# Splitting the issue of the key placements between the sync queue and ScalarE's queue in the first seven steps of a cross-attention kernel

## The chip, the cores and the metric

The kernel runs on one core of one Trainium2 chip. The metric is the device time of one execution in microseconds (us), lower is better, as the median of several runs.

## The reference, cut to what matters

One layer of a small perceiver: cross-attention of 128 queries to 12,544 keys, then a linear attention, a causal self-attention and a mixture of 8 experts, all on 128 rows of width 256. Only the first part bears on the change:

```python
q = query_states @ Wq.T + bq        # 128 x 256
k = key_value_states @ Wk.T + bk    # 12544 x 256
v = key_value_states @ Wv.T + bv
# 16 heads of 16
scores = jnp.einsum('bhqd,bhkd->bhqk', q, k)
attn = jax.nn.softmax(scores, axis=-1)
ctx = jnp.einsum('bhqk,bhkd->bhqd', attn, v)
```

## The kernel before, in words

Each engine has one program, written out by hand, and the engines meet at semaphores; every queue works in order. The keys are worked through in 49 steps (`NS`) of 256 keys (`SK`). `t` counts the rounds of the main loop: in round t TensorE computes the maximum scores of step t (`max_scores`, L568) and, `LAG` = 5 rounds later, the real scores (`scores`, L592) and the weighted values (L608). Rounds 0 to 4 therefore have no real scores, no exponentials and no weighted values yet. Projections run ahead: the values of step t+2 (`values`, L551) and the keys of step t+3 (`keys`, L540) are interleaved in round t.

Numbers are split in two parts, a high and a low one, so that a pass in fp32r keeps the precision. The way of the keys of step n is this:

- `context_high` (ScalarE, L361) and `context_low` (GpSimd, L314) split the context of step n in two parts. TensorE projects it into `k_bank`. In round t it stops before its sixth `max_scores` matmul for the low part of the context of step t+3 (`cl_ready`).
- `keys_high` (ScalarE, L371) and `keys_low` (VectorE, L907) write the high and the low part of the keys to `kst[n % 2]`, 128 partitions: rows 0 to 63 belong to the even heads (a = 0), rows 64 to 127 to the odd ones (a = 1).
- `keys_place` (L232 to L244) moves them by DMA into `kT[n % 7]`, where the 16 dimensions of eight head pairs lie on 16 partitions: for each half a three DMAs, of parts high, low, high, to partitions 64a, 64a+16 and 64a+32 on. A DMA moves 128 KB, so a step takes six of them, 768 KB. They all count up `kt_load{n % 2}`, and 96 of it mean that a step is placed.

`kst` has two buffers: `keys_high(n)` waits until the placement of step n-2 has landed. `max_scores` of step n waits for the placement of step n (`keys_placed`, in rounds before 5; from then on it stands in front of `scores`, L591). The placement also waits until GpSimd has filled its buffer of `kT` with ones (`key_ones`, L320, `pool_kt`), and from step 7 on until the scores that read the buffer before are done. VectorE reduces each of the eight pairs of maximum scores (`step_max`, L923), with `keys_low(t + 2)` between the second and the third. ScalarE's order in rounds 0 to 4 is `keys_high(t + 2)`, `values_out(t + 2)` (L381, rounds 0 to 3), `context_high(t + 4)`. The sync queue's (SP's) order in a round is one load of context (`ctx_load`, L230, 256 KB from HBM), after every fourth step the rows of the maxima (`max_rows`, L255), and `keys_place(t + 2)`.

Of the kernel before, what the change touches and what calls it, by code (L numbers as in the profile page):

```python
# [5 lines left out]
F32 = mybir.dt.float32  # L6
# [10 lines left out]
HD = D // H  # L17
# [7 lines left out]
LAG = BS + 1  # L25
LAST = NS - 1 + LAG
RING = 7
# [29 lines left out]
def last_step(b):  # L57
    return min(b * BS + BS, NS) - 1
# [46 lines left out]
def perceiver_layer(nc, dr, out):  # L105
    ctx = ExitStack()
    with ctx:
# [3 lines left out]
        S = {n: ctx.enter_context(nc.semaphore(n)) for n in COUNTING + ONCE + LOADS + ["dve_chain"]}  # L111
# [28 lines left out]
        def place(name, shape, dt=F32):  # L140
            size = 4
            for n in shape[1:]:
                size *= n
            h = nc.alloc_sbuf_tensor_at(name, shape, dt, offset=at[0])
            at[0] += (size + 31) // 32 * 32
            assert at[0] <= arena_end, (name, at[0] - arena_end)
            return h

        kT = place("kT", [P, RING, PAIRS, SK], F32R)
# [11 lines left out]
        kst = [place(f"kst{i}", [P, 2, 2 * SK], F32R) for i in range(2)]  # L161
# [60 lines left out]
        def _(sp):  # L222
# [9 lines left out]
            def keys_place(n):  # L232


                sp.wait_ge(S["kl_ready"], n + 1)
                sp.wait_ge(S["pool_kt"], min(n + 1, RING))
                if n >= RING:
                    sp.wait_ge(S["sc_done"], 8 * (n - RING) + 8)
                for a in range(2):
                    for seg, part in enumerate((0, 1, 0)):  # L240
                        row = 64 * a + HD * seg
                        sp.dma_start(kT[row:row + HD, n % RING, :, :].bitcast(F32).rearrange("d (i t) k -> d i (t k)", t=2),  # L242
                                     kst[n % 2][64 * a:64 * a + 64, part, :].bitcast(F32)
                                     ).then_inc(S[f"kt_load{n % 2}"], 16)  # L244
# [27 lines left out]
            for t in range(-2, NS + 1):  # L272
                if CRING <= t + 6 < NS:
                    ctx_load(t + 6)
                for b in range(NB):
                    if t == last_step(b) + 1:
                        max_rows(b)
                if t + 2 < NS:
                    keys_place(t + 2)
                if t == LAG:  # L280
                    sp.dma_start(biases[:, early:], dr["biases"][early:].partition_broadcast(P)).then_inc(S["ld_small"], 16)
                    sp.dma_start(router[:, :, :], dr["router"].rearrange("(c p) n -> p c n", p=P)).then_inc(S["ld_small"], 16)
                    sp.dma_start(freqs[:, :], dr["freqs"][0:P, :]).then_inc(S["ld_small"], 16)
                    sp.dma_start(const[:, P:], dr["const"][:, P:]).then_inc(S["ld_small"], 16)
                if t == NS - 2:

                    sp.wait_ge(S["v_done"], 2 * NS)
                    for name in WEIGHTS[3:]:
                        sp.dma_start(*weight(name)).then_inc(S["ld_tail"], 16)
# [65 lines left out]
        def _(act):  # L355
            def context_high(n):

                act.wait_ge(S[f"ld_ctx{n % CRING}"], 16 * (n // CRING) + 16)
                if n >= 2:
                    act.wait_ge(S["v_done"], 2 * (n - 2) + 2)  # L360
                act.activation(cparts[n % 2][:, 0, :, :], ctxT[n % CRING][:, :, :], ACT.Copy  # L361
                               ).then_inc(S["ch_ready"], 1)

            def keys_high(n):


                act.wait_ge(S["k_done"], n + 1)
                if n >= 2:
                    act.wait_ge(S[f"kt_load{n % 2}"], 96 * (n // 2))
                for t in range(2):  # L370
                    last = act.activation(kst[n % 2][:, 0, t * SK:(t + 1) * SK], k_bank[:, t * SK:(t + 1) * SK],  # L371
                                          ACT.Identity, bias=kbias[:, t:t + 1])
                last.then_inc(S["kh_ready"], 1)

            def values_out(n):


                act.wait_ge(S["v_done"], 2 * n + 2)
                if n >= VRING:
                    act.wait_ge(S["pv_done"], 2 * (n - VRING) + 2)  # L380
                act.activation(val[:, n % VRING, :, :, 0:HD].rearrange("p j h d -> p (j h) d"),  # L381
                               v_bank[:, :].rearrange("p (g d) -> p g d", d=HD), ACT.Copy).then_inc(S["val_ready"], 1)

            def exponential(n, q):


                k = 8 * n + q
                act.wait_ge(S["sc_done"], k + 1)
                if k >= PROBS:
                    act.wait_ge(S["pv_done"], (k - PROBS) // GROUPS + 1)  # L390
                act.activation(probs[k % PROBS][:, :, :], sc_bank[k % 3][:, :].rearrange("p (h q) -> p h q", q=P),  # L391
                               ACT.Exp).then_inc(S["exp_ready"], 1)

            def part_out(b):

                act.wait_ge(S["pv_done"], 2 * last_step(b) + 2)
                act.activation(parts[:, b, :], pv_bank[:, :], ACT.Copy).then_inc(S["part_ready"], 1)
# [7 lines left out]
            keys_high(0)  # L405
            act.wait_ge(S["ld_v"], 16)
            act.activation(wv[:, 0, :, :], w["xv"][:, :, :], ACT.Copy).then_inc(S["act_wkvh"], 1)
            keys_high(1)
            act.wait_ge(S["pool_setup"], 1)
            act.wait_ge(S["pe_qT"], 2)  # L410
# [4 lines left out]
            last.then_inc(S["act_q0"], 1)  # L415
            values_out(0)
            context_high(2)
            values_out(1)
            context_high(3)
            for t in range(LAST + 2):  # L420
                for q in range(8):
                    n = t - LAG
                    if 0 <= n < NS:
                        exponential(n, q)
                    if q == 0 and t + 2 < NS:
                        keys_high(t + 2)
                    if q == 5 and t + 2 <= LAG:
                        values_out(t + 2)
                    if q == 5 and t + 4 < NS:
                        context_high(t + 4)  # L430
                    if q == 2:
                        for b in range(NB):
                            if n - 1 == last_step(b):
                                part_out(b)
                    if t == NS + 1 and q == 2:

                        act.wait_ge(S["dve_dmax"], 1)
                        act.activation(bmax[:, :, :], bmax[:, :, :], ACT.Exp).then_inc(S["act_bw"], 1)
# [841 lines left out]
```

## Time and profile before

| | us |
|---|---|
| median of 3 runs | 580.96 |
| lowest, highest | 579.13, 583.05 |
| the profiled execution, its own time | 582.39 |
| span of the profiled execution | 580.60 |

The profiled execution is 1.43 us above the median, within the range of the three runs, and 1.79 us of it lie outside the span. Times in the rows count from the start of the span. PE is TensorE's matmuls, PEld its weight loads, DVE VectorE, ACT ScalarE, POOL GpSimd, SPq the sync queue. Round 0 begins at 21.36 us, round 5 at 54.15 us, and the last round of the key loop ends near 472 us.

### The profile page before, as it was taken

Reading aid. Unit: us, or ns where it says so; the run is one execution under the profiler, and the core shown is the slowest. Engines: PE = TensorE matmul, PEld = TensorE weight load, DVE = VectorE, ACT = ScalarE, POOL = GpSimd, SP = SyncE. Lnnn points to the kernel's source line nnn. Section 1 sums busy time; section 2 is a strip of 40 time slices with the busy share of each in tenths; the row PEclk is TensorE's granted clock in tenths of the full one; section 3 lists DMA queues with packets and bytes.
Section 4 is the critical chain, followed back from the end, with each engine's and each line's share of the span. In section 5 each row is a group of like instructions: output and inputs, shape, how many; then the busy total and the mean of one; then the engine's idle time right before and its main releaser. Section 6 shows DMA issues by size and latency. Waiting matters only on the chain.

```text
span 580.6 us, 15874 instructions
## 1 busy us (share of the span) xinstructions
PE 548.3 (94%) x6517; PEld 507.2 (87%) x6517; DVE 421.7 (73%) x804; ACT 331.4 (57%) x636; POOL 91.8 (16%) x75
## 2 busy tenths in 40 slices
PE   7888989999999999999999999999989998768897
PEld 7777989999999999999999999999977897736686
DVE  5699868778778778787787787787773247866674
ACT  3423747667667667667666676676666740062463
POOL 7741101111011011011011110110000000015000
PEclk9999999999999999999999999999999999988899
DMA  6999996766877877876768768777483029900000
GB/s 193 151 162 151 190 147 103 119 125 117 127 118 116 126 121 114 131 121 114 130 119 121 124 117 127 118 114 101 89 163 101 3 98 371 374 29 1 1 0 9
DMA packets 44651, 70.46 MB, mean 121 GB/s; under 512 B 6788, under 2 KB 15140, under 8 KB 44452
## 3 DMA queue, kind: packets, MB, share of 16 engines
q1 hardware_dynamic: 44580, 69.47, 64.8%
q8 instruction: 50, 0.82, 0.8%
q14 instruction: 21, 0.17, 0.1%
HBM read 30.56 MB, written 0.13 MB: 53 GB/s over the span
## 4 chain that ended last, share of the span: by engine, by line
PE 78%; DVE 10%; DMA 6%; SPq 3%; ACT 2%; issue 1%; DVEq 0%; ACTq 0%
PE bank L592 17%; PE bank L608 15%; PE bank L568 14%; PE bank L551 10%; PE bank L540 10%; DMA kT<-kst 5%; PE bank L811 3%; PE bank L827 3%; SPq L242 2%; DVE stepmax L923 2%; PE bank L616 1%; PE bank L630 1%; DMA ctxT<-in_ctxT 1%; PE bank L520 1%; DVE kst L907 1%
## 5 line engine op out<-in xcount | busy, mean ns | idle before, releaser
L923 DVE TENSOR_REDUCE stepmax<-bank 128x2 f32<-128x512 f32 x392 | 262.9, 687 | 91.6 <-PE bank L568 68.5
L391 ACT ACTIVATE probs<-bank 128x512 f32<-128x512 f32 x392 | 230.8, 599 | 141.9 <-PE bank L592 137.5
L592 PE MATMUL bank<-qmat,kT 128*128 128x256 f32 x784 | 163.5, 293 | 4.5 <-DMA kT<-kst 3.0
L568 PE MATMUL bank<-kT,qM 128*128 128x256 f32 x784 | 161.1, 287 | 4.9 <-DMA kT<-kst 2.6
L592 PEld LDWEIGHTS bank<-qmat,kT 128*128 128x128 f32 x784 | 120.3, 191 | 18.4 <-issue 10.1
L568 PEld LDWEIGHTS bank<-kT,qM 128*128 128x128 f32 x784 | 121.4, 191 | 8.9 <-DVE stepmax L923 4.5
L314 POOL TENSOR_TENSOR cparts<-ctxT,cparts 128x512 fp32r<-128x512 f32 x49 | 63.1, 1288 | 326.2 <-ACT cparts L361 326.2
L540 PE MATMUL bank<-cparts,wk 128*128 128x256 f32 x588 | 101.1, 283 | 1.6 <-DVE kst L907 1.3
L551 PE MATMUL bank<-wv,cparts 128*128 128x256 f32 x588 | 101.9, 284 | 0.7 <-ACT val L381 0.7
L608 PE MATMUL bank<-probs,val 128*17 128x128 f32 x3136 | 95.1, 273 | 0.0
L608 PEld LDWEIGHTS bank<-probs,val 128*17 128x17 f32 x3136 | 81.4, 97 | 6.5
L540 PEld LDWEIGHTS bank<-cparts,wk 128*128 128x128 f32 x588 | 83.8, 192 | 2.3 <-POOL cparts L314 2.1
L551 PEld LDWEIGHTS bank<-wv,cparts 128*128 128x128 f32 x588 | 83.9, 191 | 0.9 <-ACT val L381 0.9
L371 ACT ACTIVATE kst<-bank,kbias 128x256 fp32r<-128x256 f32 x98 | 40.8, 472 | 14.1 <-DMA kT<-kst 11.9
L907 DVE SCALAR_TENSOR_TENSOR kst<-bank,kbias,kst 128x256 fp32r<-128x256 f32 x98 | 42.5, 475 | 3.8 <-ACT kst L371 3.8
L361 ACT ACTIVATE cparts<-ctxT 128x512 fp32r<-128x512 f32 x49 | 30.5, 622 | 6.1 <-PE bank L551 3.3
L917 DVE COPY val<-bank 128x512 f32<-128x512 f32 x43 | 29.2, 680 | 0.0
L350 POOL TENSOR_TENSOR low<-w,high 128x512 fp32r<-128x512 f32 x8 | 10.0, 1292 | 111.9 <-ACT high L464 111.9
L811 PE MATMUL bank<-high,tparts 128*128 128x512 f32 x64 | 19.6, 428 | 0.2 <-DVE tparts L1148 0.2
L616 PE MATMUL bank<-const 128*128 128x128 f32 x136 | 19.2, 289 | 0.0
L1187 DVE TENSOR_TENSOR low<-w,high 128x1024 f32 (+1 forms) x12 | 14.7, 1221 | 5.9 <-ACT high L464 5.9
L616 PEld LDWEIGHTS bank<-const 128*128 128x128 f32 x136 | 18.2, 204 | 0.3
(188 smaller groups left out, 323.4 us busy)
## 6 DMA issues: line engine op xcount, KB each, us to landing
kT<-kst SPq DMA_DIRECT2D x294, 128.0 KB, 4.6
ctxT<-in_ctxT SPq DMA_DIRECT2D x49, 256.0 KB, 5.4
w<-in_w SPq DMA_DIRECT2D x24, 512.0 KB, 10.1
bias<-in_biases SPq DMA_DIRECT2D x1, 1024.0 KB, 6.7
qmat<-maxT SPq DMA_DIRECT2D x26, 8.0 KB
w_xk<-in_w_xk SPq DMA_DIRECT2D x1, 256.0 KB, 3.4
w_xq<-in_w_xq SPq DMA_DIRECT2D x1, 256.0 KB, 3.5
bias<-in_biases SPq DMA_DIRECT2D x1, 256.0 KB, 5.4
```

Of the source, the lines that this page charges most:

```text
L314: pool.tensor_tensor(cparts[n % 2][:, 1, :, :], ctxT[n % CRING][:, :, :], cparts[n % 2][:, 0, :, :].bitcast(F32), ALU.subtract).then_inc(S ...
L371: last = act.activation(kst[n % 2][:, 0, t * SK:(t + 1) * SK], k_bank[:, t * SK:(t + 1) * SK], ACT.Identity, bias=kbias[:, t:t + 1])
L391: act.activation(probs[k % PROBS][:, :, :], sc_bank[k % 3][:, :].rearrange("p (h q) -> p h q", q=P), ACT.Exp).then_inc(S["exp_ready"], 1)
L540: last = pe.matmul(k_bank[:, t * SK:(t + 1) * SK], wk[:, pw, c, t * P:(t + 1) * P], cparts[n % 2][:, pc, c, :], start=(i == 0), stop=(i == 5))
L551: last = pe.matmul(v_bank[:, j * D:(j + 1) * D], cparts[n % 2][:, pc, c, j * P:(j + 1) * P], wv[:, pw, c, :], start=(i == 0), stop=(i == 5))
L568: last = pe.matmul(mx_bank[p % 2][:, a * SK:(a + 1) * SK], qM[:, p, a, :], kT[:, n % RING, p, :], start=True, stop=True)
L592: last = pe.matmul(sc_bank[k % 3][:, i * 2 * P:(i + 1) * 2 * P], kT[:, n % RING, p, j * P:(j + 1) * P], qmat[b % 2][:, p, :, :], start=Tru ...
L608: last = pe.matmul(pv_bank[32 * r:32 * r + VW, g * P:(g + 1) * P], val[:, n % VRING, j, GH * g + r, :], probs[(GROUPS * ch + g) % PROBS][: ...
L616: pe.matmul(B[6][:, 0:P], ident, ident, start=True, stop=True)
L811: last = pe.matmul(B[2 * which + i][:, :], tparts[:, a, c, :], weights, start=(n == 0), stop=(n == len(products) - 1))
L907: last = dve.scalar_tensor_tensor(kst[n % 2][:, 1, cols], k_bank[:, cols], kbias[:, t:t + 1], kst[n % 2][:, 0, cols].bitcast(F32), ALU.add ...
L923: dve.tensor_reduce(stepmax[:, n % BS, 2 * p:2 * p + 2], mx_bank[p % 2][:, :].rearrange("p (a k) -> p a k", a=2), AX_X, ALU.max).then_inc( ...
```

## The change

In the placements of steps 0 to 6, the three DMAs of the odd heads (a = 1) are issued by ScalarE's queue and the three of the even heads stay on the sync queue. From step 7 on the sync queue issues all six as before. Bytes, shapes, destinations and semaphore counts are the same. On ScalarE the new function stands between activations: for step 0 after the copy of the value weights (L407), for step 1 after `context_high(2)`, and for steps 2 to 6 in rounds 0 to 4 behind `keys_high(t + 2)` and ahead of `values_out(t + 2)` and `context_high(t + 4)`. It waits for `kl_ready` and `pool_kt`, as the sync queue does.

```diff
@@ keys_place, sync queue
-                for a in range(2):
+                for a in range(1 if n < LAG + 2 else 2):
@@ ScalarE
+            def keys_place_half(n):
+                act.wait_ge(S["kl_ready"], n + 1)
+                act.wait_ge(S["pool_kt"], min(n + 1, RING))
+                for seg, part in enumerate((0, 1, 0)):
+                    row = 64 + HD * seg
+                    act.dma_start(kT[row:row + HD, n % RING, :, :].bitcast(F32).rearrange("d (i t) k -> d i (t k)", t=2),
+                                  kst[n % 2][64:128, part, :].bitcast(F32)).then_inc(S[f"kt_load{n % 2}"], 16)
@@ ScalarE, before the loop
             act.activation(wv[:, 0, :, :], w["xv"][:, :, :], ACT.Copy).then_inc(S["act_wkvh"], 1)
+            keys_place_half(0)
             keys_high(1)
...
             context_high(2)
+            keys_place_half(1)
             values_out(1)
@@ ScalarE, in the loop
                     if q == 0 and t + 2 < NS:
                         keys_high(t + 2)
+                    if q == 2 and t < LAG:
+                        keys_place_half(t + 2)
                     if q == 5 and t + 2 <= LAG:
                         values_out(t + 2)
```

## Rows read from the trace of the kernel before

**Rows 1.** The page: span, busy shares, and the strips in 40 slices.

```profile
span 580.6 us, 15874 instructions
PE 548.3 (94%) x6517; PEld 507.2 (87%) x6517; DVE 421.7 (73%) x804; ACT 331.4 (57%) x636; POOL 91.8 (16%) x75
...
PE   7888989999999999999999999999989998768897
...
PEclk9999999999999999999999999999999999988899
```

**Rows 2.** Busy time in stretches: a weight load, rounds 0 to 4, a late round.

```profile
core 0: us, PE busy (x) PEld busy (x) DVE busy (x) ACT busy (x) POOL busy (x), PEclk, DMA share, GB/s
8.00:10.00 2.00, 1.91 (x16) 1.75 (x15) 0.00 (x0) 0.23 (x1) 1.93 (x2) 1.00 1.05 377
...
21.36:28.20 6.84, 5.45 (x40) 4.98 (x41) 5.84 (x10) 1.90 (x4) 6.84 (x5) 1.00 1.08 153
28.20:34.95 6.75, 5.49 (x40) 5.02 (x40) 5.85 (x10) 1.96 (x4) 5.28 (x4) 1.00 1.06 155
34.95:41.16 6.21, 5.49 (x40) 5.01 (x40) 5.66 (x10) 1.95 (x4) 1.54 (x2) 1.00 1.08 170
41.16:47.62 6.46, 5.49 (x41) 5.00 (x41) 6.06 (x12) 1.96 (x4) 1.29 (x1) 1.00 1.08 166
47.62:54.15 6.53, 5.56 (x41) 5.18 (x42) 6.14 (x15) 1.47 (x3) 1.29 (x1) 1.00 0.87 140
204.47:213.25 8.78, 8.78 (x123) 8.44 (x122) 6.72 (x12) 5.80 (x12) 1.29 (x2) 1.00 0.80 122
```

**Rows 3.** The chain that ended last, 12 to 80 us: start, us, what.

```profile
17.31 0.55 SPq L242
...
21.11 7.04 DMA kT<-kst
...
28.74 1.29 DVE stepmax L923 x2
30.03 0.79 DVE kst L907 x2
...
34.00 7.12 DMA kT<-kst
...
43.77 3.78 DVE stepmax L923 x6
...
73.20 7.73 DMA kT<-kst
```

**Rows 4.** Timeline of round 1 and the edges of its neighbours: start, us; idle before in brackets.

```profile
28.24 0.84 ACT L371 ACTIVATE kst<-bank,kbias 128x256 fp32r<-128x256 f32 x2 [3.02 <-DMA kT<-kst]
28.74 1.29 DVE L923 TENSOR_REDUCE stepmax<-bank 128x2 f32<-128x512 f32 x2 [1.03 <-PE bank L568]
29.95 0.87 DVE L907 SCALAR_TENSOR_TENSOR kst<-bank,kbias,kst 128x256 fp32r<-128x256 f32 x2
30.84 3.83 SPq L242 DMA_DIRECT2D kT<-kst  x6
30.98 0.60 ACT L381 ACTIVATE val<-bank 128x512 f32<-128x512 f32 x1 [1.90 <-PE bank L551]
31.48 0.62 ACT L361 ACTIVATE cparts<-ctxT 128x512 fp32r<-128x512 f32 x1
32.17 1.28 POOL L314 TENSOR_TENSOR cparts<-ctxT,cparts 128x512 fp32r<-128x512 f32 x1 [1.47 <-ACT cparts L361]
34.95 0.50 PE L568 MATMUL bank<-kT,qM 128*128 128x256 f32 x2 [0.74 <-DMA kT<-kst]
35.49 1.29 DVE L923 TENSOR_REDUCE stepmax<-bank 128x2 f32<-128x512 f32 x2 [0.91 <-PE bank L568]
36.25 0.49 PE L568 MATMUL bank<-kT,qM 128*128 128x256 f32 x2
41.70 1.29 DVE L923 TENSOR_REDUCE stepmax<-bank 128x2 f32<-128x512 f32 x2 [0.36 <-PE bank L568]
```

**Rows 5.** The tile kst, 15 to 55 us: issue ns min/median/max; landing.

```profile
L242 SPq DMA_DIRECT2D kT<-kst x36: 547/598/1720, 14.7 to 54.6; - x36
...
DMA to landing us min/median/max: 3.3/5.9/7.8
```

## Prediction

> **What bounds the kernel now.** I read the page first. TensorE's matmuls are busy for 94% of the span, at the full granted clock in all but the last slices, and the one visibly thinner part of the key loop is its beginning [rows 1]. Then the windows by round. A late round takes 8.78 us with TensorE busy for all of it; there a placement is hidden and the change does nothing, since it ends with step 6. Rounds 0 to 4 are 6.84, 6.75, 6.21, 6.46 and 6.53 us long with TensorE busy for only about 5.5 us of each, so something else sets them. The column before the last tells what: the DMA engines have a share above 1 in rounds 0 to 3, so they never run dry, at 153, 155, 170 and 166 GB/s, and fall to 0.87 in round 4 [rows 2].
>
> The chain of waits gives the order. It goes from the issue of step 1's placement to its landing, 7.04 us after the last of six issues; then over TensorE to two reductions and `keys_low(3)` on VectorE, to the issue of step 3's placement, and to its landing, 7.12 us after the last issue. From 41.7 us on it stays on VectorE [rows 3]. So in rounds 0 and 1 the bound is a loop: placement lands, `keys_high` and `keys_low` fill the freed buffer, the next placement is issued and lands. From round 3 it is VectorE, busy 6.06 us of 6.46 [rows 2].
>
> The timeline prices it. VectorE stands idle for want of a placed step 1.03 us before round 1, 0.91 before round 2 and 0.36 before round 3 [rows 4], 2.30 us in all. That is the most that earlier landings in these rounds can return; below it VectorE's eight reductions and two halves of `keys_low`, 5.66 to 5.85 us a round [rows 2], take over.
>
> **The change part by part.** Removed from the sync queue: 7 x 3 = 21 issues at a median 0.60 us [rows 5]. Six in a row take 3.83 us [rows 4], so with three on each queue the last one is issued some 1.9 us earlier. But the landing isn't the issue plus a constant. One issue of this kind lands 3.3 us after it when nothing is ahead, 5.9 in the median and up to 7.8 [rows 5], and the last of a step takes 7 in the chain [rows 3]: the difference is a queue in front of the DMA engines. While their share is above 1, issuing earlier only makes the queue longer. At nothing, therefore, I put the 1.9 us itself; what covers it is the backlog. In round 4, where the share is 0.87, the cover is gone, but there VectorE is the bound, and the placement of step 6 isn't needed before round 6.
>
> What can change is the pace of the DMA engines. The same engines moved 377 GB/s when they loaded weights from HBM to all partitions, and 153 to 155 when three quarters of their bytes were placements (768 KB of 1 MB in a round), at the same share [rows 2]. So in a placement they are busy waiting: its writes go to 16 partitions at a time, those of one half a for three DMAs on end. With two queues, placements to partitions 0 to 47 and to 64 to 111 are in flight together, and a context load on the sync queue can run beside odd-head placements. The low end of this effect is nothing. The high end is that the stalls end, 2.30 us, for which a round of 6.84 us must shrink to about 5.9, 16% more pace. The nearest rows are rounds 2 and 3, with the same work at 170 and 166 GB/s. I take 170 for rounds 0 and 1: 6.84 x 153/170 = 6.16, saves 0.68; 6.75 x 155/170 = 6.15, saves 0.60; and of round 2's 0.36 I count 0.3, as it then meets VectorE. Sum 1.6 us.
>
> Added to ScalarE: 21 issues and a wait for `keys_low` in each of rounds 0 to 4. Queued behind it are `values_out(t + 2)` and `context_high(t + 4)`; TensorE waits for the first at the start of the next round, and GpSimd, and through it TensorE, for the second. No row shows an issue on ScalarE. By the issues on the sync queue it costs 0.55 to 1.72 us, median 0.60 [rows 5]; I take the median, because both queues do the same instruction, so 3 x 0.64 with the gaps, 1.9 us. In round 1 ScalarE would be through at 30.84 + 1.9 = 32.7 instead of beginning `values_out` at 30.98, and end it at 33.3, `context_high` at 34.0, and GpSimd's half at 35.3. TensorE wants the values at about 35.2, behind the first maximum scores of the next round, and the context part in the third pair, which begins at 36.25 [rows 4]. Both are ready, by 1.9 and about 1.1 us, and with a next round that starts 0.4 us earlier still by 1.5 and 0.7. ScalarE has the room: it is busy 1.96 us of 6.75 [rows 2]. Cost nothing; the cover is TensorE's own work, and it breaks at about 1.0 us an issue (below).
>
> Steps 0 and 1 are placed before the loop. Half of step 0 goes out from ScalarE with `keys_high(1)` behind it, and half of step 1 behind `context_high(2)`, some 0.6 us after the sync queue's half, which still is before the time at which the sixth issue went out. Nothing for either. Rounds from 5 on: ScalarE and the sync queue have their old programs, TensorE is the bound, and what was won or lost before shifts them as a whole. The late landing in the chain at 73 us is that of step 8 behind a group of small loads [rows 3]; it is untouched and moves with the rest.
>
> Sum: -1.6 us. The profiled execution would take 582.39 - 1.6 = 580.8; on the median of the runs, 1.43 lower, it is 580.96 - 1.6 = 579.4.
>
> **The Trainium skill on this.** "SBUF — State Buffer", section "Can I just issue two DMAs to hit both halves?", says no: all DMAs run on the same 16 engines, and two at once, one at partition 0 and one at 64, gained only 6%. "DMA: Bandwidth & Descriptors", section "Issuing engines are not separate DMA queues", adds that a second issuing engine saves only the sequencer's time. Their plain form is the second case below. The trace supports the first half of it (one saturated set of engines) and can't show the other, as all its DMAs but instruction loads are in one queue. With the 6% the rounds would be 6.45 and 6.37 us, an estimate of about 1.1 us saved in place of 1.6.
>
> **The rivals.** (a) Faster pace, the forecast: 579.4, from 578.4 with all 2.3 us and a little at the start of round 0, to 580.4 with a third of it. (b) Hidden anyway: two rings, one set of engines, the same pace, and the placements land when they did. For it: a share above 1 from 21 to 47 us. Against: 377 against 153 GB/s at that share. It gives 581.0. (c) Slower, through ScalarE: two queues that issue at the same moment may take turns, so that an issue takes twice as long, 1.28 us, and three 3.84. Then ScalarE is free at 34.68, the context's high part ends at 35.9 and the low one at 37.25, and TensorE, due at about 36.5 for the second matmul of the third pair, waits 0.8 us in each of the rounds 1 to 4; with `keys_high` of the next round late by as much, that is 3.4 us, 584.4. It decides from (36.5 - 30.84 - 0.60 - 0.62 - 1.29 - 0.1) / 3 = 1.0 us an issue. At the longest single issue, 1.72 us [rows 5], it would be 2.1 us a round, 589.4. For it: the 1.72 exists. Against: it is one of 36, the median is 0.60.
>
> **How the numbers follow.** (a) 0.50, (b) 0.28, (c) 0.20, of which 0.04 at or above the longer price, and 0.02 for what I haven't thought of. One per cent is 5.8 us, about what a measurement of this kernel can tell from no change, as the three runs are 3.9 us apart. (a) and (b) lie wholly within it, and (c) at its likely price too. So faster by over 1% 0.02 (the last case), within 1% 0.94, slower 0.04. The range goes from (a)'s upper gain, less 1.1 us for the scatter of a median, to (c)'s likely price: 577.3 to 584.4; outside it are the long form of (c) and scatter.
>
> **What would show it.** In the profile after, rounds 0 and 1 should be near 6.15 us, with 165 to 175 GB/s in them, and VectorE's idle time before rounds 1, 2 and 3 should sum to under 1 us instead of 2.30. ScalarE's three issues should take about 1.9 us, and `context_low` should still end before the third pair of the next round. The time from the last issue to the landing should rise where (b) holds, to about 9 us, with rounds of 6.8 and 6.75. Under (c) issues on both queues take 1.2 us or more and TensorE's wait for `cparts` (GpSimd, L314) appears in rounds 1 to 4. I would be wrong beyond the range if ScalarE's issues blocked on the backlog of the DMA engines, or if rounds from 5 on changed their 8.78 us.

## The result, and the profile after

| | before | after |
|---|---|---|
| median, us | 582.35 (579.07 to 585.60, 16 runs) | 585.86 (583.13 to 589.74, 16 runs) |
| ratio, 95% interval | | 1.007 (1.0049 to 1.0091) |
| span of the profiled execution, us | 580.60 | 586.20 |

The change costs 0.7% by the ratio; the two medians are 3.5 us apart. The forecast was a gain of 1.6 us. The profiled execution of after, 587.97 us, lies 2.1 us above its own median, so its 5.6 us of longer span are more than the change costs.

The windows by round, of the changed kernel; columns as in [rows 2]. The windows are rounds 0 to 5, then the stretch from round 8's first scores to round 9's, then a late round:

```profile
21.09:27.93 6.84, 5.53 (x42) 4.98 (x41) 5.85 (x10) 1.96 (x4) 5.91 (x5) 1.00 1.07 154
27.93:34.40 6.47, 5.50 (x40) 5.00 (x40) 5.85 (x10) 1.96 (x4) 4.37 (x4) 1.00 1.06 158
34.40:40.34 5.94, 5.41 (x41) 5.04 (x41) 5.39 (x10) 1.96 (x4) 2.57 (x2) 1.00 1.09 178
40.34:46.72 6.38, 5.52 (x41) 5.04 (x40) 6.30 (x11) 1.96 (x4) 1.70 (x2) 1.00 1.07 173
46.72:56.47 9.75, 5.80 (x42) 5.16 (x42) 7.66 (x16) 1.47 (x3) 2.17 (x2) 1.00 1.06 168
56.47:64.78 8.31, 8.31 (x57) 8.31 (x57) 6.08 (x11) 5.61 (x11) 0.89 (x1) 0.79 0.19 36
82.34:95.01 12.67, 10.53 (x123) 9.82 (x122) 7.60 (x18) 5.91 (x12) 1.28 (x2) 0.87 0.48 97
209.00:217.78 8.78, 8.78 (x123) 8.44 (x122) 6.73 (x12) 5.80 (x12) 1.29 (x2) 1.00 0.80 123
```

Rounds 1, 2 and 3 are 0.28, 0.27 and 0.08 us shorter than in [rows 2], and a late round is unchanged. Round 4 is 9.75 us in place of 6.53, and its DMA share is 1.06 in place of 0.87. Round 5 is 8.31 us with TensorE busy for all of it, at a mean granted clock of 0.79; before, the same stretch is

```profile
54.15:61.36 7.21, 7.11 (x59) 6.81 (x57) 6.93 (x13) 5.61 (x11) 0.89 (x1) 1.00 0.95 141
79.14:89.83 10.69, 9.14 (x123) 8.60 (x122) 7.61 (x18) 5.81 (x12) 1.29 (x2) 1.00 0.57 111
```

and the second line is before's stretch of round 8, 1.98 us shorter than after's. So +3.22 us in round 4, +1.10 in round 5, +1.98 in round 8, and less than a microsecond back in rounds 1 to 3.

The chain that ended last, of the changed kernel, names what came in (start, us, what). The first line is the landing of step 2's placement, where the chain of [rows 3] had landings of 7.04 us (step 1) and 7.12 us (step 3); the last line answers to its 7.73:

```profile
25.12 9.24 DMA kT<-kst
...
50.72 0.74 SPq L255
51.51 4.92 DMA qmat<-maxT
56.47 0.50 PE bank L606 x2
...
76.38 8.34 DMA kT<-kst
```

`qmat<-maxT` are the rows of the block maxima, two DMAs of 8 KB issued by `max_rows` (L255), without which `scores` of round 5 can't start. They aren't in the chain before. The timeline of round 4 of the changed kernel:

```profile
49.94 1.85 ACTq L391 DMA_DIRECT2D kT<-kst  x3
50.72 1.44 SPq L255 DMA_DIRECT2D qmat<-maxT  x2
52.26 1.87 SPq L242 DMA_DIRECT2D kT<-kst  x3
...
56.47 0.50 PE L606 MATMUL bank<-qmat,kT 128*128 128x256 f32 x2 [2.57 <-DMA qmat<-maxT]
```

and of the kernel before (the window asked for ends at 55 us, so the last placement shows four of its six issues):

```profile
51.13 1.43 SPq L255 DMA_DIRECT2D qmat<-maxT  x2
52.66 2.51 SPq L242 DMA_DIRECT2D kT<-kst  x4
54.15 0.40 PE L592 MATMUL bank<-qmat,kT 128*128 128x256 f32 x2
```

Before, step 6's placement stood behind the rows on the one queue, though it was ready about 0.8 us before they were: `keys_low(6)` ends at 50.32 us, and the issue of the rows begins at 51.13. With two queues ScalarE issues its half, 384 KB, from 49.94 us on, all three DMAs of it before the second row DMA at 51.5. That row DMA lands 4.92 us after its issue, where before it took at most the 2.3 us to TensorE's start at 54.15, and TensorE waits 2.57 us.

One more line differs in round 4. VectorE's and GpSimd's rows, first before, then after:

```profile
45.13 1.29 POOL L314 TENSOR_TENSOR cparts<-ctxT,cparts 128x512 fp32r<-128x512 f32 x1 [4.92 <-ACT cparts L361]
47.87 0.17 DVE L937 TENSOR_SCALAR maxparts<-curmax 128x16 fp32r<-128x16 f32 x1
```

```profile
46.32 1.28 POOL L314 TENSOR_TENSOR cparts<-ctxT,cparts 128x512 fp32r<-128x512 f32 x1 [4.61 <-ACT cparts L361]
47.03 0.61 DVE L951 TENSOR_SCALAR maxparts<-curmax 128x16 fp32r<-128x16 f32 x1
```

The same small operation takes 0.61 in place of 0.17 us and ends at 47.64, when GpSimd's ends (47.60). ScalarE's issues pushed GpSimd's part 1.2 us later, so that the two now run at the same time. That row and the wait for the rows of the maxima make up 3.0 of round 4's 3.22 us.

ScalarE's issues themselves, and the time to landing of both queues' placements (compare [rows 5]):

```profile
L242 SPq DMA_DIRECT2D kT<-kst x21: 552/595/683, 12.2 to 53.5; - x21
L391 ACTq DMA_DIRECT2D kT<-kst x21: 554/634/871, 12.2 to 51.2; - x21
...
DMA to landing us min/median/max: 3.5/6.5/9.2
```

### The profile page after: what moved, and what is told of

The parts are those of the page before. It is cut to its first block, busy times and chain, and to the rows that moved or that the text cites. A ratio compares the mean times of both kernels' runs of the same rounds, so it can differ in the third digit from the quotient of the medians.

```text
span 586.2 us, 15881 instructions
## 1 busy us (share of the span) xinstructions
PE 551.2 (94%) x6517; PEld 510.5 (87%) x6517; DVE 422.8 (72%) x804; ACT 331.5 (57%) x636; POOL 92.1 (16%) x75
## 4 chain that ended last, share of the span: by engine, by line
PE 77%; DVE 10%; DMA 7%; SPq 2%; ACT 2%; issue 2%; ACTq 0%; POOL 0%; DVEq 0%
PE bank L606 17%; PE bank L622 15%; PE bank L582 14%; PE bank L565 10%; PE bank L554 10%; DMA kT<-kst 4%; PE bank L825 3%; PE bank L841 2%; DVE stepmax L937 2%; DMA qmat<-maxT 2%; PE bank L630 1%; PE bank L644 1%; SPq L242 1%; DMA ctxT<-in_ctxT 1%; PE bank L534 1%
## 5 line engine op out<-in xcount | busy, mean ns | idle before, releaser
L565 PE MATMUL bank<-wv,cparts 128*128 128x256 f32 x588 | 103.3, 287 | 0.7 <-ACT val L381 0.7
L565 PEld LDWEIGHTS bank<-wv,cparts 128*128 128x128 f32 x588 | 85.2, 194 | 0.9 <-ACT val L381 0.9
```

Source lines behind the costliest of these rows:

```text
L565: last = pe.matmul(v_bank[:, j * D:(j + 1) * D], cparts[n % 2][:, pc, c, j * P:(j + 1) * P], wv[:, pw, c, :], start=(i == 0), stop=(i == 5))
```

## The experiments

Three readings are taken from each profile: the time from round 0's first maximum scores to round 5's first scores (**lead-in**), TensorE's wait for the rows of the maxima (**rows**), and the time from round 7's first maximum scores to round 8's, which holds the wait for step 8's placement; the expectations call it the length of round 8 (**round 8**). It ends ahead of any slower clock behind that wait. Ratios are to the kernel before on the same chip, but not all rows stem from one chip.

| kernel | lead-in | rows | round 8 | ratio (95%) |
|---|---|---|---|---|
| before, four profiles | 32.79, 32.79, 32.70, 32.79 | none | 10.58, 9.46, 9.51, 9.46 | |
| changed, three profiles | 35.38, 34.55, 34.12 | 2.57, 3.36, 2.5 | 11.34, 11.17, 11.17 | 1.007 (1.0049 to 1.0091) |
| split of steps 0 to 5, two profiles | 32.70, 32.78 | none | 10.86, 10.80 | 1.0027 (1.0005 to 1.0049) |
| split of step 6 only | 35.81 | 2.93 | 11.52 | 1.0116 (1.0084 to 1.0149) |
| half of step 6 later | 33.08 | 1.15 | 11.05 | 1.0061 (1.0038 to 1.0083) |
| one queue, rows behind step 6 | 37.81 | 5.00 | 9.77 | 1.0136 (1.0106 to 1.0166) |
| changed, idle matmuls | 38.13 | hidden | 11.50 | 1.0097 (1.0059 to 1.0135) |
| before, small loads late | 32.76 | none | 8.78 | 0.9982 (0.9956 to 1.0009) |
| split 0 to 5, small loads late | 32.70 | none | 8.78 | 0.9984 (0.9959 to 1.0008) |
| changed, small loads late | 35.37 | 2.58 | 8.78 | 1.0023 (0.999 to 1.0055) |
| split 0 to 5, small loads late, half of step 5 later | 32.33 | none | 8.78 | 0.9961 (0.9941 to 0.9982) |
| changed, padded | 35.70 | 2.6 | 10.95 | 1.0042 (1.0015 to 1.007) |
| changed, const later | 35.47 | 2.4 | 11.18 | 1.0082 (1.0048 to 1.0115) |
| split 0 to 5, const later | 32.88 | none | 10.73 | 1.0023 (0.999 to 1.0056) |

**Split of steps 0 to 5 only.**

```diff
-                for a in range(1 if n < LAG + 2 else 2):
+                for a in range(1 if n < LAG + 1 else 2):
...
-                    if q == 2 and t < LAG:
+                    if q == 2 and t < LAG - 1:
```

> The split kept for steps 0 to 5; all six DMAs of step 6's placement back on the sync queue, behind the rows of the maxima. Theory A (the loss comes from the odd half of step 6, which now stands in the DMA engines ahead of the rows of the maxima, L255, that round 5 waits for): no wait for these rows in front of round 5, which begins near 53.3 us in place of 56.5; total 0.9 us under the kernel before, ratio 0.997 to 1.000. Rival B (the second queue as such makes small transfers of the sync queue late): the wait for the rows stays at 1 us or more and the ratio is 1.003 to 1.007. Rival C (ScalarE's issues in rounds 0 to 4 cost the time): ratio 1.003 or more with no wait for the rows.

```profile
53.94 0.40 PE L606 MATMUL bank<-qmat,kT 128*128 128x256 f32 x2
```

The wait for the rows is gone, and round 5 begins at 53.94 us. That speaks for theory A against B. But ScalarE's queue has nothing to issue in round 4 of this kernel, so a form of B in which both queues must be in use at that moment is left. C had named a ratio of 1.003 or more without a wait; 1.0027 (1.0005 to 1.0049) doesn't exclude it, and the next kernel and those with the small loads moved decide on it. But the total isn't under the kernel before, it is 1.6 us over: of the expected 0.9 us at most 0.1 has arrived at the start of round 5, and something is lost in round 8.

**Split of step 6 only.**

```diff
+                for a in range(1 if n == LAG + 1 else 2):
...
-            keys_place_half(0)
-            keys_place_half(1)
...
+                    if q == 2 and t == LAG - 1:
```

> Only step 6's placement split, steps 0 to 5 as before. Theory A: the full loss and none of the small gain, a wait of 2 to 3.5 us for the rows of the maxima in front of round 5, ratio 1.006 to 1.012. Rival C (ScalarE's issues in rounds 0 to 3): ratio 1.000 to 1.002.

The full loss, by the one half placement of round 4, and far from the 1.000 to 1.002 of rival C. The line of its timeline:

```profile
58.05 0.51 PE L604 MATMUL bank<-qmat,kT 128*128 128x256 f32 x2 [2.93 <-DMA qmat<-maxT]
```

**ScalarE's half of step 6 behind `context_high(8)`.**

```diff
-                    if q == 2 and t < LAG:
+                    if q == 2 and t < LAG - 1:
                         keys_place_half(t + 2)
...
                         context_high(t + 4)
+                    if q == 5 and t == LAG - 1:
+                        keys_place_half(t + 2)
```

> All seven placements split, but in round 4 ScalarE issues its half of step 6 behind context_high(8), so about 52.5 us, behind the sync queue's issue of the rows of the maxima (50.7 to 52.2 us). Theory A: no wait or under 0.5 us for the rows, ratio 0.997 to 1.001, as with the split of steps 0 to 5 alone. Rival B (a second queue in use makes the rows late): a wait of 1 us or more, ratio 1.003 to 1.007.

```profile
50.39 1.44 SPq L255 DMA_DIRECT2D qmat<-maxT  x2
51.17 1.87 ACTq L391 DMA_DIRECT2D kT<-kst  x3
...
54.71 0.50 PE L608 MATMUL bank<-qmat,kT 128*128 128x256 f32 x2 [1.15 <-DMA qmat<-maxT]
```

In between. By the numbers on record this is B's case: a wait of 1 us or more and a ratio of 1.003 to 1.007, against 1.15 us and 1.0061. But the edit didn't make the kernel that both theories were asked about. The half went out at 51.17 us, not 52.5, while the rows were issued from 50.39 to 51.83, so it stood beside the second row DMA and not behind both; that DMA lands 3.5 us after its issue, in place of 4.9. The kernel doesn't separate A from B, and the others must. Its profile doesn't explain its ratio either: the lead-in is 0.3 us longer and round 8 0.5 to 1.6 us, where 1.0061 are 3.5 us.

**One queue, with step 6's placement ahead of the rows.**

```diff
             for t in range(-2, NS + 1):
...
+                if t == LAG - 1:
+                    keys_place(t + 2)
                 for b in range(NB):
                     if t == last_step(b) + 1:
                         max_rows(b)
-                if t + 2 < NS:
+                if t + 2 < NS and t != LAG - 1:
                     keys_place(t + 2)
```

> The kernel before, one queue only, with step 6's placement issued ahead of the rows of the maxima in round 4. Theory A (order in front of the DMA engines, not the queue): the rows land 4 us or more later than before, the wait in front of round 5 is 3.5 to 6 us, ratio 1.007 to 1.014. Rival B (it takes a second queue): under 1.5 us of wait, ratio 1.000 to 1.003.

```profile
59.70 0.80 PE L594 MATMUL bank<-qmat,kT 128*128 128x256 f32 x2 [5.00 <-DMA qmat<-maxT]
```

The chain of the same kernel:

```profile
54.58 0.74 SPq L255
55.36 4.30 DMA qmat<-maxT
```

Theory A: the order alone makes the wait, and it needs no second queue. The 5.00 us have two parts, though. The six issues of the placement, 50.74 to 54.53 us, hold back the issue of the rows by more than 3 us; and the second row DMA, once issued, lands 4.30 us later, in place of at most 2.3. Only the second part is a queue in front of the DMA engines, and it is no longer with six DMAs ahead than with ScalarE's three: 4.92 us in the changed kernel, 5.28 in the one that splits step 6 only.

**The changed kernel with 16 idle matmuls ahead of round 5's wait.**

```diff
                 if n == first_step(b) and q == 0:
+                    if b == 0:
+                        keep_busy(16)
                     pe.wait_ge(S["max_rows"], 32 * (b + 1))
```

> The changed kernel, with 16 idle matmuls of 128x128 on TensorE in front of round 5's wait for the rows of the maxima, so that TensorE isn't idle in it. Theory A2 (part of the loss is the clock, which fell to half for 3.4 us behind this wait): the wait stays, but the granted clock stays at 1.00 from 54 to 66 us, round 5 lasts 7.2 us in place of 8.2, ratio about 1.004 to 1.006 in place of 1.007. Rival (the clock costs nothing): no change from the changed kernel, 1.007.

The window of round 5 in that kernel:

```profile
59.46:66.40 6.94, 6.94 (x59) 6.85 (x58) 5.89 (x11) 5.50 (x11) 0.89 (x1) 1.00 0.00 0
```

The clock stays at its upper level (2.4 GHz), and the round lasts 6.94 in place of 8.31 us. That gives the price of the lower clock, theory A2, but not its cure. In the changed kernel's third profile TensorE waited 2.46 us, without idle matmuls, and the clock didn't fall either:

```profile
54.92:61.89 6.97, 6.97 (x57) 6.88 (x57) 5.89 (x11) 5.51 (x11) 0.89 (x1) 1.00 0.25 43
```

So that the idle matmuls kept the clock up isn't shown. The total is a miss. The idle matmuls took 3.73 us, over a microsecond more than the 2.57 us that they were to cover, and in this profile the clock had already fallen in round 4, behind two waits of 0.93 and 0.97 us.

**The four small loads moved from round 5 to round 44**, in three kernels: before, split of steps 0 to 5, changed.

```diff
-                if t == LAG:
+                if t == NS - 5:
                     sp.dma_start(biases[:, early:], ...
```

> The kernel before, one queue, with the four small loads moved from round 5 to round 44. All theories: it saves the wait of 1.55 us in front of round 8's scores and at times a fall of the clock, ratio 0.994 to 0.998. It is the yardstick for the two runs with the same loads moved.

> The split for steps 0 to 5, and the four small loads of round 5 (1.2 MB) moved to round 44. Theory A3 (what the split of steps 0 to 5 loses against the kernel before lies in round 8, where step 8's placement lands late behind the small loads and the clock falls): no wait for a placement in round 8, granted clock 1.00 from 80 to 95 us, ratio to the kernel before 0.993 to 0.997, and equal to or up to 0.001 under the kernel before with the same loads moved. Rival (the split itself costs time in the first rounds or after): 0.002 or more above that kernel.

> The changed kernel with the four small loads moved to round 44. Theory A (the rows of the maxima land late behind ScalarE's half of step 6): against the yardstick the loss at round 5 stays, 2.3 us of late start and 1.0 of lower clock, so 0.005 to 0.006 above the kernel before with the same loads moved, and the further 1.5 to 2 us of round 8 are gone. Rival (all of the loss is round 8's): equal to the yardstick.

Round 8's wait is gone in all three. The split of steps 0 to 5 is now equal to the single queue (0.9984 and 0.9982): its loss lay in round 8, theory A3. Both lie above what was expected (0.993 to 0.997 for the split, 0.994 to 0.998 for the single queue). The changed kernel stays 0.0041 above the yardstick, 2.4 us, a little less than the 0.005 to 0.006 expected; that is the measure of what the rows cost, and the rest of its 0.007 would be round 8's. It is a rough one, as the two intervals overlap; in the profiles of these two kernels the lead-in is 2.6 us longer and round 5 0.9 us. Taken alone, 0.9982 isn't told from no change.

**The same with ScalarE's half of step 5 behind `context_high(7)`.**

```diff
-                    if q == 2 and t < LAG - 1:
+                    if q == 2 and t < LAG - 2:
                         keys_place_half(t + 2)
...
                         context_high(t + 4)
+                    if q == 5 and t == LAG - 2:
+                        keys_place_half(t + 2)
```

> The split for steps 0 to 5 with the small loads in round 44, and in round 3 ScalarE issues its half of step 5 behind context_high(7), no longer ahead of it. Theory D (in round 4 VectorE's first step of the maxima in two parts takes 0.60 us in place of 0.17 because GpSimd's context_low, which ScalarE's issues made later, runs at the same moment): GpSimd is through before it, the operation takes 0.17 us again, and the time from round 0 to round 5's scores falls from 32.7 to about 32.3 us. Rival (the 0.60 has another cause): it stays at 0.60. The total is at most 0.001 under the same kernel without this edit, too little for the ratio to tell.

```profile
44.26 1.29 POOL L314 TENSOR_TENSOR cparts<-ctxT,cparts 128x512 fp32r<-128x512 f32 x1 [2.63 <-ACT cparts L361]
47.02 0.17 DVE L953 TENSOR_SCALAR maxparts<-curmax 128x16 fp32r<-128x16 f32 x1
```

GpSimd is through at 45.6, the operation takes 0.17 us again, and the lead-in falls to 32.33 us: theory D. The Trainium skill, "SBUF — State Buffer", section "Who interferes with whom", says that VectorE and GpSimd share a pair of ports which, in VectorE's two-port modes, one of them holds for a whole instruction while the other is blocked. The changed kernel's rows agree with it in that VectorE's operation ends when GpSimd's does, at 47.6 us; in which mode it ran, no run here shows. This kernel has the lowest median of all, 580.05 us, 0.9961. That its ratio lies 0.002 under the one without the edit is more than 0.4 us explain; the two stem from different chips, and the difference is within the intervals.

**More profiles of the kernels.**

> The kernel before, unchanged, for a second profile. All theories: no wait for the rows of the maxima, round 0 to round 5's scores 32.8 us within 0.1. Theory A3 (round 8's wait is near the point at which the clock falls, and varies from run to run): a wait of 1.2 to 2.0 us for step 8's placement.

> The split for steps 0 to 5, unchanged, for a second profile. Theory A3: round 0 to round 5's scores 32.7 us, and a wait of 1.5 to 2.2 us in round 8 with or without a fall of the clock behind it.

> The changed kernel, unchanged, for a second profile. Theory A: a wait of 2.3 to 2.9 us for the rows of the maxima in front of round 5, round 0 to round 5's scores 35.2 to 35.6 us, a stretch of 3.4 us at the half clock behind it.

> The kernel before, for a third profile. If round 8's length is systematic by kernel: 9.4 to 10.6 us. If it is scatter: anything from 9.4 to 11.5.

> The kernel before, for a fourth profile, as in the one above: 9.4 to 10.6 us for round 8 if systematic, up to 11.5 if scatter.

> The changed kernel, for a third profile. Systematic: round 8 of 10.8 to 11.5 us, and a wait for the rows of the maxima of 2.3 us or more. Scatter: round 8 from 9.4 on.

The lead-ins of before agree within 0.1 us. Round 8 isn't scatter alone: 9.46 to 10.58 us in before's four, 11.17 to 11.34 in the changed kernel's three. Before's later profiles lie under the expected wait of 1.2 us or more (0.42 us in the first of them). The changed kernel's second profile began round 0 at 24.9 us, and the third at 20.8; their lead-ins, 34.55 and 34.12, are under the expected 35.2, since rounds 0 and 1 took 5.82 to 6.27 us in them. The wait for the rows is there each time; its 3.36 us in the second profile are above the expected 2.3 to 2.9, and round 5 took 9.47 us there, at a mean granted clock of 0.68.

**What makes round 8 longer.** Single-queue profiles have one long issue on the sync queue where most of the others have none. In before's second profile and in the changed kernel's first, the issue of the last small load is

```profile
67.30 1.69 SPq L284 DMA_DIRECT2D const<-in_const  x1
```

and

```profile
69.89 0.43 SPq L284 DMA_DIRECT2D const<-in_const  x1
```

In before's first profile, the one with 10.58 us, the long issue is that of the context load behind it, 1.79 us. Two tries to bring this back, first 21 idle waits on the sync queue, then a wait that holds the load back by about as much:

```diff
+                if n < LAG + 2:
+                    for _ in range(3):
+                        sp.wait_ge(S["kl_ready"], n + 1)
```

```diff
+                    sp.wait_ge(S["sc_done"], 14)
                     sp.dma_start(const[:, P:], dr["const"][:, P:]).then_inc(S["ld_small"], 16)
```

> The changed kernel with three more waits (already met) behind each of the seven split placements on the sync queue, 21 in all. Theory E (round 8 is late because the sync queue's program, 21 instructions shorter, no longer has its long issue of 1.7 us among the small loads): the long issue comes back among them and round 8 lasts 9.5 to 10.6 us. Rival (the place in the program is without effect): round 8 stays at 10.8 us or more and the ratio at 1.007.

> The changed kernel, in which the sync queue waits for the sixth score group of round 6 (sc_done 14) before the last of the four small loads (const), so that it and the context load behind it go out about 1.5 us later, near 71.5 and 72.0 us, as the single-queue kernels do by their long issue. Theory F (it is the time of these two issues): round 8 lasts 9.4 to 10.0 us in place of 10.8 to 11.5, and the ratio falls from 1.007 to about 1.004. Rival (only a companion): round 8 stays at 10.8 us or more.

> The split for steps 0 to 5 with the same wait ahead of the load of const. Theory F: round 8 of 9.4 to 10.0 us, no fall of the clock behind it, ratio 1.000 or a little under, in place of 1.0027. Rival: round 8 of 10.8 us and a ratio near 1.003.

The padding left the issue at 0.43 us and round 8 at 10.95, so it tested nothing but that the number of waits isn't it. With the load held back, to 70.63 and 68.69 us, round 8 stays at 11.18 and 10.73. Theory F falls: the late issue is only a companion. The kernel with idle matmuls says the same; it had a long issue of its own, 1.94 us, one small load earlier, and a round 8 of 11.50 us. Why a kernel that used ScalarE's queue earlier has step 8's placement later, when that queue is idle, stays open.

## Why the prediction was wrong

**The bound of rounds 0 to 3** was read right. The placements' landing and VectorE set them, and rounds 1 and 2 are shorter, by 0.28 and 0.27 us. VectorE's idle time before rounds 1, 2 and 3 is 1.09, 0.62 and nothing, 1.7 us, where I had asked for under 1 in place of 2.30.

**The pace of the DMA engines** rose, by less than I took: 158 GB/s in round 1 against 155, 178 against 170 in round 2, and round 0 not at all (154, 6.84 us). In place of 1.6 us the four rounds gave 0.63 (26.26 to 25.63 us from round 0's start to round 4's). That is nearer to the 6% of the Trainium skill's "SBUF — State Buffer", section "Can I just issue two DMAs to hit both halves?", than to my 170 GB/s for every round. I took rounds 2 and 3 as a measure of what a second queue could do, when they ran at 170 and 166 GB/s on one. The size isn't the same in every execution: in the changed kernel's third profile rounds 0 and 1 moved 160 and 165 GB/s, and the four rounds took 24.32 us, a gain above the forecast's. Of step 2's placement in round 0 the last issue came 1.7 us earlier (1.49 us behind the first; a single queue needs 3.16 for six) and landed 9.24 us later, in place of about 7.8, near the 9 us of the case "hidden anyway".

**ScalarE's room** was right where I looked: an issue takes 0.63 us, three 2.1, `context_low` of round 1 ended at 35.2 as worked out (35.3), and rival (c), whose sign was right, didn't come by its mechanism. That (c)'s price, 3.4 us, is close to the 3.5 us between the medians is chance. What I didn't ask was whom a later GpSimd would meet: 0.44 us in round 4, by the row of `maxparts`, which used up most of the gain.

**The step that failed** is the sentence on round 4: "there VectorE is the bound, and the placement of step 6 isn't needed before round 6". Both halves are true and beside the point. The question was not when step 6's placement is needed, but what it was queued behind. On the single queue it stood behind `max_rows(0)`, which round 5 needs within 3 us; on ScalarE's queue it doesn't. I had costed the split as an issue that comes earlier at no cost, while the DMA engines had a share above 1 up to round 3. The runs show its place and price: with nothing else split, 2.93 us of wait and 1.0116; with the order alone changed on one queue, 5.00 us, of which over 3 are later issues, and 1.0136; with step 6 not split, no wait. How the DMA engines share their time between two queues, no run here isolates. I had listed step 6's placement and the order of the sync queue, and never put `max_rows` in the sum: it had no row in what I read, since before nobody waited for it.

**The clock** was missing too. TensorE at rest for 2.57 us was followed by a mean granted clock of 0.79 over 8.31 us, about 3.5 us at the half, which made round 5 1.10 us longer than before's, and 1.3 to 1.4 us longer than behind waits after which the clock stayed up (6.94 to 6.97 us). It is not the sure price of such a wait: behind 2.46 us in the changed kernel's third profile and 2.43 in the one with the later const the clock stayed at 1.00. Round 8's waits for the placement were 1.7 to 2.5 us in the kernels that had used ScalarE's queue, and the clock fell behind five of these eleven, of 1.8 to 2.3 us; it fell behind none of before's, of 0.4 to 1.6.

**"What was won or lost before shifts them as a whole"** was wrong for round 8. Against the yardstick with the small loads moved, about 2.4 of the 4.1 us (0.7%) are rounds 4 and 5, and the other 1.7 are round 8's; the intervals leave room for another division. What makes round 8 longer is open, as told above.

**The range and the chances.** 584.4 was the price of one mechanism of loss; the measured median lies above it by 1.5 us, of which 1.4 is the kernel before itself, whose median over 16 runs is 582.35 in place of 580.96. "Within 1%" held; the direction didn't.

## What to carry to other kernels

A single queue is also an order. When part of a transfer moves to a second queue, list everything that it used to stand behind, above all small transfers on which a stage waits, and ask who gets in front in the DMA engines now; 16 KB of rows behind 384 KB of keys cost more than all the earlier landings gave. A producer that is made later without making anybody wait can still collide with a third engine, so follow it to the end. Where a wait of TensorE is added, price a slower clock behind it as a case of its own: here it came behind some waits and not behind others of the same length.

## What the runs showed of the hardware

- Two queues, one to partitions 0 to 47 and one to 64 to 111, together moved 154 to 178 GB/s in rounds 0 to 2 of one profile and 160 to 175 in another, against 153 to 170 of a single queue.
- A small VectorE operation on 128x16 took 0.61 in place of 0.17 us while GpSimd ran beside it, in every profile in which they met, and 0.17 again when they were parted.
- After 2.57 us of wait TensorE's granted clock fell to the half (1.2 GHz) for about 3.5 us of the next round, which took 8.31 us; after 2.46 us in another execution of the same kernel it stayed at 1.00, and the round took 6.97 us.
- A row DMA of 8 KB landed 4.92 and 5.28 us after its issue with three DMAs of 128 KB issued ahead of it on another queue, and 4.30 us with six ahead on its own; with no such DMA just ahead it took at most 2.3 us.
- Single runs of one kernel differ by up to 6.6 us, and they do so with the granted clock of the whole run: of the changed kernel's 16, the one at 0.994 took 583.13 us, and the three at 0.980 took 587.98, 588.48 and 589.74.
